# Band attention's opening on one core: context rows are added behind the first two tiles' scores, and one tile's statistics stand behind the first maximum

## The reference, cut to what matters

```
x = x + xattn(layernorm(x), ctx, ctx, mask)
# xattn:
scores = einsum('bqe,bke->bqk', query, key) / sqrt(512)
band = abs(idx[:, None] - idx[None, :]) <= 128
scores = where(band & mask, scores, -1e9)
out = einsum('bqk,bke->bqe', softmax(scores), value)
```

## Time and profile before

| | us |
|---|---|
| median of 3 runs | 2896.57 (2893.86 to 2897.49) |
| the profiled execution | 2895.68 |
| its span, first to last instruction | 2893.8 |
| outside the span | 1.88 |
| TensorE busy in the span | 2867.4 (99%) |
| VectorE busy | 2063.2 (71%) |
| ScalarE, GpSimd busy | 1344.3, 1325.5 (46%, 46%) |

### The profile page before, as it was taken

One profiled execution on the slowest core, in us unless ns is written; L12 is line 12 of the kernel. 1 busy time (PEld: TensorE's weight loads), 2 busy tenths in 40 slices (PEclk: granted clock), 3 DMA queues, 4 the chain that ended last, 5 costly groups with the idle time before them and its releaser, 6 DMA issues. The chain is left out here.

```text
span 2893.8 us, 53018 instructions
## 1 busy us (share of the span) xinstructions
PE 2867.4 (99%) x20256; PEld 2529.8 (87%) x20256; DVE 2063.2 (71%) x4135; ACT 1344.3 (46%) x2807; POOL 1325.5 (46%) x1406
## 2 busy tenths in 40 slices
PE   9999999999999999999999999999999999999999
PEld 7887888888889999999998888888879999999998
DVE  8987677776677666766657767776676766676765
ACT  7875556565554222222235556655554332223231
POOL 7867677776642211122105677776662223222221
PEclk9999999999999999999999999999999999999999
DMA  6753233322047777777783223332127777777775
GB/s 218 238 188 104 96 104 105 121 92 81 30 178 289 277 272 265 272 265 254 259 314 115 95 94 108 110 117 92 49 68 284 275 279 273 274 286 281 282 272 187
DMA packets 184897, 547.02 MB, mean 189 GB/s; under 512 B 26678, under 2 KB 82490, under 8 KB 162116
## 3 DMA queue, kind: packets, MB, share of 16 engines
q1 hardware_dynamic: 184500, 543.57, 53.1%
q10 hardware_dynamic: 144, 0.07, 0.0%
HBM read 447.11 MB, written 93.70 MB: 187 GB/s over the span
## 5 line engine op out<-in xcount | busy, mean ns | idle before, releaser
L1247 PE MATMUL quad<-fhT_f,slot_f 128*128 128x256 f32 (+1 forms) x2088 | 594.8, 285 | 0.2 <-DVE sums_f L2062 0.2
L1248 PE MATMUL quad<-fhT_f,slot_f 128*128 128x256 f32 (+1 forms) x2088 | 590.0, 283 | 0.0
L1249 PE MATMUL quad<-fhT_f,slot_f 128*128 128x256 f32 (+1 forms) x2088 | 589.8, 282 | 0.0
L1247 PEld LDWEIGHTS quad<-fhT_f,slot_f 128*128 128x128 f32 (+1 forms) x2088 | 392.5, 188 | 0.4 <-DVE sums_f L2062 0.4
L1249 PEld LDWEIGHTS quad<-fhT_f,slot_f 128*128 128x128 f32 (+1 forms) x2088 | 392.7, 188 | 0.0
L1248 PEld LDWEIGHTS quad<-fhT_f,slot_f 128*128 128x128 f32 (+1 forms) x2088 | 392.7, 188 | 0.0
L1666 ACT ACTIVATE gate_f_raw<-gate_f_raw,bias_f 128x512 f32<-128x512 f32 (+1 forms) x176 | 127.2, 722 | 551.2 <-DVE gate_f_raw L2085 551.2
L2173 POOL TENSOR_SCALAR stats<-stats 128x1 f32<-128x1 f32 x64 | 35.6, 556 | 693.4 <-DVE stats L2025 692.5
L1534 ACT ACTIVATE lprob<-lprob,small 128x384 f32<-128x384 f32 (+2 forms) x512 | 288.7, 566 | 137.4 <-DVE small L1885 137.4
L2290 POOL TENSOR_TENSOR turned_qk<-with_cos,with_sin 128x256 f32<-128x256 f32 x252 | 186.9, 762 | 333.0 <-DVE with_sin L1909 237.3
L1000 PE MATMUL bank_pair<-wqkv_h,hT 128*128 128x512 f32 x992 | 319.0, 403 | 0.0
(11 more groups left out here) (296 smaller groups left out, 7436.1 us busy)
## 6 DMA issues: line engine op xcount, KB each, us to landing
slot_f<-parts SPq DMA_DIRECT2D x160, 1792.0 KB, 7.6
slot_f<-parts SPq DMA_DIRECT2D x16, 1190.0 KB, 5.2
s_in<-stream SPq DMA_DIRECT2D x128, 128.0 KB, 2.8
s_res<-stream SPq DMA_DIRECT2D x64, 256.0 KB, 2.9
stream<-a_out SPq DMA_DIRECT2D x64, 256.0 KB, 2.0
res_f<-stream SPq DMA_DIRECT2D x63, 256.0 KB, 7.3
h_in_f<-stream SPq DMA_DIRECT2D x112, 128.0 KB, 5.5
parts<-part_high SPq DMA_DIRECT2D x20, 512.0 KB, 2.6
```

The lines of the kernel that those rows point to most:

```text
L1247: e.matmul(bank[0:n, :], high, row_high, start=c == 0, stop=False)
L1248: e.matmul(bank[0:n, :], high, row_low, start=False, stop=False)
L1249: ins = e.matmul(bank[0:n, :], low, row_high, start=False, stop=c == 1)
```

## The change

Three things move, all in the first steps of the band phase.

- TensorE adds the context rows of tile 0 in step 3, no longer in step 2, and behind the scores of tile 0; those of tile 2 move from step 3 to step 4, behind the scores of tile 1.
- VectorE takes the statistics of tile 3 at the end of step 3, behind the maximum of tile 0's scores, no longer at the step's beginning.
- VectorE makes `ctx_l` of tiles 0 to 3 in steps 3 to 6, no longer 2 to 5.

```
@@ tensor_program, band() @@
-                if s == 2:
-                    band_add_rows(0)
                 if 0 <= s - 3 < TILES:
                     band_scores(s - 3)
                 if s == 3:
+                    band_add_rows(0)
                     band_add_rows(1)
+                if s == 4:
                     band_add_rows(2)
-                if s == 4:
                     band_add_rows(3)
@@ vector_program, band() @@
-                if s < TILES:
+                if s < TILES and s != 3:
                     band_query_statistics(s)
...
                 if 0 <= s - 3 < TILES:
                     band_exponents(s - 3)
-                if 0 <= s - 2 < SUM_AHEAD:
-                    band_first_ctx_low(s - 2)
+                if s == 3:
+                    band_query_statistics(s)
+                if 0 <= s - 3 < SUM_AHEAD:
+                    band_first_ctx_low(s - 3)
```

## The result

| | us |
|---|---|
| changed kernel, median of 15 runs | 2900.54 (2898.02 to 2903.57) |
| kernel before, median of 15 runs beside them | 2895.28 (2893.41 to 2897.49) |
| ratio, 95% interval | 1.002 (1.0012 to 1.0027) |
| profiled execution: before, after | 2895.68, 2901.70 |
| its span: before, after | 2893.8, 2899.9 |

The change costs 5.3 us by the medians and 6.0 us between the two profiled executions. The time is 0.4 us from the forecast. The sum behind it was not: 3.57 us against the profiled execution, where 6.0 us were found.

What follows compares the result with a forecast made beforehand. TensorE, busy 99% of the span, was taken as the bound. Terms 0.0 + 1.42 + 1.42 + 0.73 = 3.57 us gave a forecast median of 2900.1 us, range 2897.0 to 2903.0.

Steps and rivals of the forecast that it cites:

- The two added waits: TensorE before mix 1 (step 6) and mix 2 (step 7): each waits 1.42 us for VectorE's later `ctx_l`.
- the upper end with 1.73: At mix 1 and mix 2: `ctx_l` as slow as 1.73 us beside a working GpSimd, adding 1.04 to each wait.
- Mix 3: TensorE waits 0.73 us for the low part of `probT`, late through GpSimd's first `ctx_l` and ScalarE's normalising of query 6.
- After that GpSimd catches up: GpSimd behind mix 3's chain: lateness made up from its band waits, 36.0 us in 28, 1.3 each.
- The opening nets 0.0 us: TensorE up to the total: 0.85 us gained is spent on the moved addition; total at 20.23, before 20.22.
- one of the forecast's own signs of being wrong: End of the opening: the forecast is wrong if the total starts more than 0.5 us from 20.2.
- the rival that the clock stays low: TensorE's opening: low clock through first scores and two additions costs 3.3 us more, 6.9 in all, 2903.4; chance 0.06.
- None comes back: TensorE after the stalls: no lost time is regained, since step follows step without slack; sum stays 3.57 us.
- a milder rival: Later band steps: stalls come back out of 2.2 us of idle time, leaving +1.4, 2898.0; no chance of its own.
- Its sign of being wrong, shorter steps from 8 on: Band steps 8 to 31: the forecast is wrong if they are shorter than before.
- The statistics: Step 3: their move is hidden, GpSimd's sums ending at about 19.1, 1.1 us before the total wants them.
- The cover of the second `ctx_l`: Before mix 0, due 21.09: second `ctx_l` ready at 19.9, so its later place is hidden.

Runs made afterwards that it cites:

- ctx_late_only: Kernel before with only VectorE's `ctx_l` of tiles 0 to 3 moved to steps 3 to 6; 2899.13 us, +5.0, ratio 1.0015.
- own_count: Changed kernel with GpSimd counting its low parts in its own semaphore, not waiting for VectorE's fourth; 2897.16 us, +3.0, ratio 1.0011.
- early_gap: ctx_early plus three idle products on TensorE in step 2, in the gap of the moved addition; 2895.25 us, +0.3, ratio 1.0002.
- ctx_early: Changed kernel with `ctx_l` of tile 0 in step 3, tiles 1 and 2 in step 4, tile 3 in step 5; 2895.57 us, +1.4, ratio 1.0005.
- rows_only: ctx_early with the statistics of tile 3 back at the beginning of step 3; 2895.67 us, +0.7, ratio 1.0003.
- one_wait: Changed kernel with `ctx_l` of tile 0 in step 3, tiles 1 and 2 in step 4, tile 3 in step 6; 2900.54 us, +6.4, ratio 1.002.
- early_fill: ctx_early plus idle products on TensorE in steps 1 and 2 (4, 2 and 3); 2894.59 us, -0.35, ratio 1.0001.
- after_fill: Changed kernel plus idle products on TensorE in steps 1 and 2 (4, 2 and 3); 2899.21 us, +5.1, ratio 1.0018.
- stats_only: Kernel before with only the statistics of tile 3 moved behind the first maximum; 2893.45 us, -0.7, ratio 0.9997.
- stats_fill: stats_only plus six idle products on TensorE in steps 1 and 2 (4 and 2); 2894.79 us, -0.15, ratio 0.9999.
- before_fill: Kernel before plus six idle products on TensorE in steps 1 and 2 (4 and 2); 2895.80 us, +1.7, ratio 1.0005.

## Why the prediction was right, and where it was not

**The two added waits were right.** Forecast 1.42 each; 1.36 and 1.31 us of idle time, and 1.51 and 1.57 by the starts. Both had the cause named: a low part behind a maximum that needs the scores just made. VectorE's subtraction took 0.69 beside a waiting GpSimd both times, so the upper end with 1.73 did not come. ctx_late_only reproduces them without the rest of the change.

**Mix 3 was right.** Forecast 0.73 us through GpSimd, ScalarE's `xn` and both parts of `probT`; measured 0.87 of idle time and 1.08 by the starts, with `probT` as releaser. In own_count, where GpSimd is in time, the wait is gone.

**"After that GpSimd catches up" failed.** The forecast took 1.3 us a step from an average: 36.0 us of waiting in 28 waits. That average was over the whole band. Behind 36.94 GpSimd has no wait up to 70 us, yet its lateness falls only from 8.67 to 6.40 in five steps, 0.45 us a step. The kernel before shows why: in those steps, from 28.27 to 59.68, GpSimd has three waits there, of 0.75, 0.74 and 0.74 us, and those 2.23 us were all that could be made up. It was not asked who needs GpSimd next except ScalarE. `key_put` for the second batch stood in the same queue with 0.48 us to spare, and 2.08 us were lost there, the largest single wait. A full list of what GpSimd hands on between steps 6 and 12 would have shown it.

**"The opening nets 0.0 us" failed, by the clock.** The forecast let the clock rise near 11.93 as before. Windows of TensorE in the changed kernel, columns as in the earlier trace rows:

```profile
9.50:10.00 0.50, 0.00 (x0) 0.50 1.02 381
...
13.50:14.00 0.50, 0.50 (x5) 0.50 0.98 361
14.00:14.50 0.50, 0.50 (x5) 0.70 0.52 189
```

TensorE stands idle from 9.5 to 10.0, and the clock rises from 0.50 (1.2 GHz) only between 14.0 and 14.5. The scores of tile 0 take 14.47 - 11.69 = 2.78 us and not 1.64, the first maximum starts at 14.68 and not at 13.57, and the total at 21.28. A total more than 0.5 us from 20.2 was one of the forecast's own signs of being wrong. This is the mechanism of the rival that the clock stays low, in a milder form: it rises before the additions, which keep their length, and the total loses 1.06 us, not 3.3. The 13 traces and early_gap tie it to the gap. The Trainium skill (TensorE: Matmul & The Clock Gate, Part 1: The HAM clock gate) has the throttled state as what holds until activity releases it, and this trace agrees: 14.3 us behind a gap, 11.9 without one. How late the rise comes is not the gap's doing alone. In the trace of the changed kernel the low level also begins earlier, at 7.5 and not at 8.5 us, where both kernels still run the same instructions.

It also differs from one execution to the next. With the additions moved and nothing in the gap (the changed kernel, ctx_early, rows_only, own_count, one_wait) 23 of 59 executions had a mean clock of 0.998 or less; with idle products in the gap (early_gap, early_fill, after_fill) 3 of 33; with the additions in their old place and no such products (the kernel before, ctx_late_only, stats_only) 7 of 115. Such executions of the kernel before take 2896.7 in the mean, those at 0.999 2894.7. But a mean over the whole execution does not say where the clock was low. The profiled execution of ctx_early reads 0.999 with the rise at 14.7 us, and those of rows_only and own_count read 1.000 with slow scores. So it is likely, and not shown, that the moved additions make the whole time longer by a late clock; the two medians that bear on it alone, +0.7 and +1.4, do not clear their intervals.

**"None comes back" failed, to the good.** By mix 6 1.38 us of the lateness had come back, as the wait of 0.94 there vanished. The forecast held this for a milder rival, out of the 2.2 us of later idle time. Its sign of being wrong, shorter steps from 8 on, thus came for steps 8 to 10, though not for the whole: the lateness is 5.22 at mix 3 and 6.1 at the end. The wait had come from one of VectorE's small instructions, which took 1.23 us for one number per row in front of mix 6's chain. VectorE and GpSimd in the kernel before:

```profile
53.91 1.23 DVE L1762 SCALAR_TENSOR_TENSOR soft<-soft 128x1 f32<-128x1 f32 x1 [0.41 <-ACT even L1452]
```

```profile
53.84 1.28 POOL L2168 TENSOR_TENSOR ctx_sum<-ctx_sum,sum_in 128x512 f32<-128x512 f32 x1
```

VectorE in the changed kernel, in front of the same mix, and in own_count:

```profile
58.10 0.16 DVE L1761 SCALAR_TENSOR_TENSOR soft<-soft 128x1 f32<-128x1 f32 x1 [0.41 <-ACT even L1451]
```

```profile
57.51 1.21 DVE L1766 SCALAR_TENSOR_TENSOR soft<-soft 128x1 f32<-128x1 f32 x1 [0.41 <-ACT even L1456]
```

It is 1.07 us shorter. In the kernel before it ends at 55.14, just behind GpSimd's sum at 55.12, which began before it. own_count differs from the changed kernel by GpSimd's count alone, and has GpSimd's sum beside it again, the long instruction, and a wait at mix 6 (0.27). All 13 traces agree: 1.21 to 1.24 us in the nine where GpSimd's `ctx_sum` runs beside it, 0.16 in the four with a late GpSimd.

**Sum.** Opening +1.1, mix 1 +1.5, mix 2 +1.6, mix 3 +1.1, given back -1.4, mask +2.2: 6.1 by the mask product. The three terms that were missed make 1.9 net, and the three waits that were forecast came out 0.6 longer by the starts than their 3.57. That the forecast of the median is closer (0.4 us) is partly luck. It was the first median of the kernel before, 2896.57, plus 3.57. With 12 more runs that median fell by 1.3, and the medians differ by 5.3: 1.7 more than forecast, less 1.3.

**The statistics** were hidden as forecast: GpSimd's sums end at 20.19, 1.1 us before the total wants them. The cover of the second `ctx_l` was thinner than the working had it: mix 0 was put at 21.09 and not at its 20.67, and in the changed kernel it starts at 21.73, 0.15 behind that `ctx_l`, without a wait. Alone, the move of the statistics gives a median 0.7 us lower, not told from zero.

**What stays open.** Idle products brought the total forward by 0.4 to 2.5 us, but the distance to the kernel before changed, by the medians, by -1.8 (early_fill against ctx_early), -1.1 (early_gap), -0.2 (after_fill), +0.6 (stats_fill against stats_only) and +1.7 us (before_fill). Each of these is uncertain by 2 us or more, so whether an earlier opening shortens the whole is not settled. From the start of the total to the end of the span, profiled kernels with the same waits differ by up to 2.2 us (2871.4 to 2873.6 among those without any added wait), and nothing here says why.

## What to carry to other kernels

When work is moved a step later, ask of every semaphore it counts who else waits for that count: GpSimd, which needed none of the data, stood 9.3 us for it here and brought the largest stall 30 us later, through a mask row. A count of its own was worth about 2.3 us. Follow such a late queue item by item, with the margin of each thing it hands on, and never pay its lateness back with a phase's average slack; add up the waits that it really has in that stretch. Work at the head of a phase that looks like pure cost can be what lifts TensorE's clock: moving it back freed 1.7 us there, and the scores behind it lost 1.1.

## What the runs showed of the hardware

The granted clock of a window was not always what the pace said. In rows_only it reads full from the start, in this window of TensorE:

```profile
12.00:13.00 1.00, 1.00 (x7) 1.00 1.06 391
```

yet the scores of tile 0 take 2.51 us there and 1.64 in the kernel before. From start to start their products take 0.21 us each up to 13.33 and 0.12 from 13.51. So the clock was low until about 13.4, and the column did not show it; own_count is a second case (2.49 us at a column of 1.00). The pace from start to start is the safer witness.

The point of that rise moved by microseconds between kernels that differ little: about 13.4 us in rows_only, 14.3 in the changed kernel, 14.7 in ctx_early, 16.1 in one_wait. The changed kernel and one_wait have the same instructions on TensorE in the same order up to there, so the order alone doesn't set it.

An instruction of VectorE on one number per row (`soft` from `soft`, 128x1) took 0.16 us with no large GpSimd instruction beside it, and 1.21 to 1.24 us when GpSimd's sum of 128x512 had begun 0.06 to 0.08 us before it; it then ended with that sum. The subtraction of 128x512 took 0.69 us on VectorE beside a waiting GpSimd and 1.73 beside a working one.
